# Last turns of a fused attention kernel: query product first, query norm last, hand-over and final norm rearranged

## The reference, cut to what matters

```python
# x: [32, 32, 512], ctx: [32, 257, 512]; 16 heads of 32
x = x + xattn(layernorm(x), ctx, ctx, mask)          # q/k/v/o products, softmax over 257 keys
x = x + attn(layernorm(x))                           # per sequence of 32 tokens:
#   q, k, v = split(z @ Wqkv.T + bqkv)
#   q = q / sqrt(mean(q*q) + 1e-6) * qn_w            # k likewise ("head norm")
#   out = softmax(q k^T / sqrt(32)) v ; out @ Wproj.T + bproj
z = layernorm(x)
xm = mix[0]*z_before + mix[1]*z + mix[2]*z_after     # along the sequence
h = einsum('bsd,pdm->bspm', xm, W1) + b1             # 9 experts, 128 wide
paths = einsum('bspm,pmd->bspd', h, W2) + b2
choice = argmax(tanh(xm @ Wo1 + bo1) @ Wo2 + bo2)
return x + layernorm(z + paths[choice]) * gamma + beta
```

## Time and profile before

| | us |
|---|---|
| median of 3 runs (lowest to highest) | 794.52 (793.86 to 794.61) |
| profiled execution, its own time | 793.65 |
| its span, first to last instruction | 791.7 |
| PE busy in the span | 751.6 |
| DVE, ACT, POOL busy | 390.5, 335.9, 187.7 |
| mean granted TensorE clock | 0.99 |

### The profile page before, as it was taken

One profiled execution on the slowest core, in us unless ns is written; L12 is line 12 of the kernel. 1 busy time (PEld: TensorE's weight loads), 2 busy tenths in 40 slices (PEclk: granted clock), 3 DMA queues, 4 the chain that ended last, 5 costly groups with the idle time before them and its releaser, 6 DMA issues. The chain is left out here.

```text
span 791.7 us, 20456 instructions
## 1 busy us (share of the span) xinstructions
PE 751.6 (95%) x8258; PEld 587.8 (74%) x8258; DVE 390.5 (49%) x942; ACT 335.9 (42%) x690; POOL 187.7 (24%) x245
## 2 busy tenths in 40 slices
PE   5999999999999999999999999799999989999994
PEld 4777778778877877787788777677877766677673
DVE  5544434343443344243424546756667675633546
ACT  4435444443444344444435455224554545521210
POOL 0001000010010010010100202555777770692002
PEclk9999999999999999999999999999999999999998
DMA  9211110011011101101120114120000022100011
GB/s 331 71 48 55 54 55 23 33 53 53 0 53 53 53 0 53 53 1 52 53 49 4 53 53 108 66 84 3 0 0 4 2 69 80 41 1 0 1 54 53
DMA packets 9471, 37.05 MB, mean 47 GB/s; under 512 B 2633, under 2 KB 2889, under 8 KB 6482
## 3 DMA queue, kind: packets, MB, share of 16 engines
q1 hardware_dynamic: 9426, 36.42, 13.6%
HBM read 34.32 MB, written 2.10 MB: 46 GB/s over the span
## 5 line engine op out<-in xcount | busy, mean ns | idle before, releaser
L94 PE MATMUL pj<-W_hi 128*128 128x512 f32 x512 | 209.1, 408 | 9.7 <-DVE W_lo L594 9.7
L96 PE MATMUL pj<-W_lo,W_hi 128*128 128x512 f32 x512 | 201.2, 393 | 0.0
L95 PE MATMUL pj<-W_hi,W_lo 128*128 128x512 f32 x512 | 200.4, 391 | 0.0
L94 PEld LDWEIGHTS pj<-W_hi 128*128 128x128 f32 x512 | 96.8, 189 | 40.7 <-issue 22.4
L96 PEld LDWEIGHTS pj<-W_lo,W_hi 128*128 128x128 f32 x512 | 96.7, 189 | 21.4
L95 PEld LDWEIGHTS pj<-W_hi,W_lo 128*128 128x128 f32 x512 | 97.0, 189 | 17.9
L235 POOL COPY q_b<-Q_T 128x128 f32 (+1 forms) x32 | 9.3, 291 | 415.8 <-PE tp L358 348.9
L492 ACT ACTIVATE K<-pj,bk 128x512 f32<-128x512 f32 x64 | 44.1, 690 | 136.1 <-PE pj L96 136.1
L654 DVE CUSTOM_DVE_ANT_0 m_flat<-sc,mask 128x257 f32<-128x257 f32 x64 | 25.3, 425 | 115.4 <-PE tp L358 94.1
L507 ACT ACTIVATE p_flat<-m_flat,nmax 128x257 f32<-128x257 f32 x128 | 63.8, 501 | 24.5 <-DVE nmax L654 24.5
L499 ACT ACTIVATE V<-pj 128x512 f32<-128x512 f32 x64 | 38.2, 598 | 73.7 <-PE pj L96 71.8
(11 more groups left out here) (287 smaller groups left out, 1329.3 us busy)
## 6 DMA issues: line engine op xcount, KB each, us to landing
raw<-ctx_dram SPq DMA_DIRECT2D x15, 1024.0 KB, 4.8
raw<-w_dram SPq DMA_DIRECT2D x6, 768.0 KB, 4.9
raw<-w_dram SPq DMA_DIRECT2D x4, 1024.0 KB, 4.8
x_nat<-x_dram SPq DMA_DIRECT2D x2, 1024.0 KB, 11.7
out_dram<-raw SPq DMA_DIRECT2D x8, 256.0 KB, 2.1
raw<-wk_dram SPq DMA_DIRECT2D x2, 512.0 KB, 5.4
p_flat<-ctx_dram SPq DMA_DIRECT2D x2, 512.0 KB, 6.8
m_flat<-wv_dram SPq DMA_DIRECT2D x1, 1024.0 KB, 9.9
```

Of the source, the lines that this page charges most:

```text
L94: eng.matmul(out, a_hi, b_hi, start=first, stop=False)
L95: eng.matmul(out, a_lo, b_hi, start=False, stop=False)
L96: return eng.matmul(out, a_hi, b_lo, start=False, stop=last)
```

## The change

The whole change is in the second part, from 485 us on.

1. Turns 6, 7 and NT: PE makes the query product first, then `out_proj`, then the transposes of q and k. In every turn from 2 on `z2_transposes` goes ahead of `weighted_sum`, and ACT makes `z2_hi` ahead of `o_hi`.
2. DVE: in a turn `head_norm(it-1, 0)`, the query norm, goes from behind `k_evac` to the end; the `lo` half of z2 goes ahead of `v_evac`. DVE's turns are all written out, without a loop.
3. Hand-over: `wo_proj(4)` has a PSUM bank of its own, so that neither it nor `qkv(2, 0)` waits for the bank `pw[0]` to be read; the split of the fifth weight goes earlier on ACT and on DVE (from the end of turn 1 to behind `q_evac(1)`); both head norms of tile 0 go ahead of `x1_stats(2)`.
4. Gate: `xm_hi` and `xm_lo` are made tile by tile in turns 4 to 7, `xm_lo` on DVE instead of POOL, and `g_lo` likewise on DVE.
5. Start of the experts: `spread(0)` goes ahead of the last `weighted_sum`, `out_proj(NT+2)` and both last `z3_transposes` go later, `w_split(2)`, `z3_make` and `mix_parts` take other places among the hidden rows.
6. End: the last four tiles' deviations come one by one from POOL's power; tiles 4 and 6 go through ACT (scale and shift), POOL (gamma) and an addition on POOL or DVE; tiles 5 and 7 stay on DVE. Stores follow in the order 4, 5, 7, 6.
7. Some semaphores are shared by both parts, and some are gone.

```diff
-            if isinstance(t, int) and t <= LEAD + 1:
-                return (pw[0][:, :], pw[1][:, :], pa[:, 0, :], pa[:, 1, :])[t]
+            if isinstance(t, int) and t <= LEAD + 2:
+                return (pw[0][:, :], pw[1][:, :], pa[:, 0, :], pa[:, 1, :], pa[:, 2, :])[t]
...
 # PE, body(it)
                 if has(it, -LEAD):
                     wo_proj(it + LEAD)
-                if has(it, 3):
+                    if has(it, 3):
+                        out_proj(it)
+                if not has(it, -LEAD):
+                    qkv(it, 0)
                     out_proj(it)
-                if isinstance(it, int) and it == 2:
+                    qk_transposes(it)
+                elif isinstance(it, int) and it == 2:
                     qkv(it, 0)
                     qk_transposes(it)
...
+                if not isinstance(it, int) or it >= 2:
+                    z2_transposes(it)
                 if has(it, 2):
                     weighted_sum(it)
-                if not isinstance(it, int) or it >= 2:
-                    z2_transposes(it)
...
 # PE, behind the turns
+            qkv(NT, 0)
             out_proj(NT)
             qk_transposes(NT)
-            qkv(NT, 0)
             scores(NT)
...
             hidden(1)
+            spread(0)
             weighted_sum(NT + 1)
-            spread(0)
             spread(1)
-            out_proj(NT + 2)
             hidden(2)
             spread(2)
+            out_proj(NT + 2)
+            expert(RING)
             z3_transposes(NT + 1)
-            expert(RING)
+            expert(RING + 1)
             z3_transposes(NT + 2)
...
 # ACT, body(it) and behind the turns
                 eng.activation(z2_hi[:, :, :].rearrange("p c t -> p (c t)"), pt[0][:, :], ACT.Copy).then_inc(z2hi_made, 1)
+                if has(it, 2):
+                    o2_split(it)
...
+            def xm_split_tile(u):
+                cols = slice(u * P, (u + 1) * P)
+                eng.wait_ge(mix_made, u + 2)
+                eng.activation(xm_hi[:, :, cols], O_T[:, :, cols], ACT.Copy).then_inc(xmhi, 1)
...
             choice_evac(0)
             w_split(1)
-            w_split(2)
+            spread_evac(0)
             o2_split(NT + 1)
-            z3_make(NT + 1)
-            spread_evac(0)
             hidden_split(0)
             spread_evac(1)
+            z3_make(NT + 1)
             hidden_split(1)
+            w_split(2)
+            spread_evac(2)
+            hidden_split(2)
             eng.wait_ge(proj_done, NT)
             eng.activation(b2_hi, b2, ACT.Copy).then_inc(b2_split, 1)
-            z3_make(NT + 2)
-            spread_evac(2)
-            mix_parts(NT + 1)
-            hidden_split(2)
-            w_split(3)
             spread_evac(RING)
             hidden_split(RING)
-            mix_parts(NT + 2)
-            w_split(4)
+            z3_make(NT + 2)
+            mix_parts(NT + 1)
+            w_split(3)
             spread_evac(RING + 1)
             hidden_split(RING + 1)
+            w_split(4)
+            mix_parts(NT + 2)
             w_split(5)
...
+            for t in (0, 2):
+                eng.wait_ge(shift4_made, t // 2 + 1)
+                eng.activation(y(NH + t), y(NH + t), ACT.Identity, bias=shift4[:, t:t + 1],
+                               scale=rstd4[:, t:t + 1]).then_inc(normed, 1)
...
 # DVE, the last tiles
-            y_centre(1, NH - 1)
-            y_deviations()
-            for t in (2, 3, 0, 1):
-                if t < 2:
-                    eng.wait_ge(centred, 2 * t + 2)
+            y_centre(1, 3)
+            for t in (1, 3):
+                eng.wait_ge(root_step, 2 * t + 2)
                 y_end(1, t)
+            eng.wait_ge(centred, 2)
+            eng.tensor_tensor(y(NH + 2), y(NH + 2), x_nat[:, NH + 2, :], ALU.add).then_inc(fin, 1)
```

More of the change, by code:

```diff
@@ L767, with self_attention_and_experts @@
 LEAD = 2
-def self_attention_and_experts(nc, io, out, x_nat, ident, O_T, raw, W_hi, W_lo, Wp_hi, Wp_lo, bv, bo, o_b, o_first, w_in, whi, wlo, ln3):
+def self_attention_and_experts(nc, io, out, x_nat, ident, O_T, raw, W_hi, W_lo, Wp_hi, Wp_lo, bv, bo, o_b, o_first, w_in, whi, wlo, seen, ln3):
     with ExitStack() as ctx:
@@ L962, in _ @@
                     eng.dma_start(beta, row_on_all(io["beta"])).then_inc(ln_in, 16)
-            for i, t in enumerate((0, 1, 2, 3, 6, 7, 4, 5)):
-                eng.wait_ge(fin, i + 1)
+            for t in range(NH):
+                eng.wait_ge(fin, t + 1)
+                eng.dma_start(out[t], y(t)).then_inc(stored, 16)
+            eng.wait_ge(fin0, 1)
+            eng.dma_start(out[NH], y(NH)).then_inc(stored, 16)
+            for i, t in enumerate((5, 7, 6)):
+                eng.wait_ge(fin, NH + i + 1)
                 eng.dma_start(out[t], y(t)).then_inc(stored, 16)
@@ L1084, in _, with y_root, y_scale @@
                 eng.tensor_tensor(x_nat[:, t, :], x_nat[:, t, :], beta, ALU.add).then_inc(xb_made, 1)
-            for t in range(2):
-                y_t = y(NH + t)
+            def y_root(t):
+                one = slice(t, t + 1)
                 eng.wait_ge(stats_made, NH + t + 1)
-                eng.tensor_scalar(y_t, y_t, mv4[:, t, 0:1], None, ALU.subtract).then_inc(centred, 1)
-                eng.wait_ge(centred, 2 * t + 1)
-                eng.tensor_tensor(y_t, y_t, gamma, ALU.mult).then_inc(centred, 1)
+                eng.tensor_scalar(tmp4[:, one], mv4[:, t, 1:2], LN_EPS, 1.0, ALU.add, ALU.mult).then_inc(root_step, 1)
+                eng.wait_ge(root_step, 2 * t + 1)
+                eng.tensor_tensor(rstd4[:, one], tmp4[:, one], power[:, one], ALU.pow).then_inc(root_step, 1)
+                eng.wait_ge(root_step, 2 * t + 2)
+                if t in (0, 2):
+                    eng.tensor_scalar(shift4[:, one], mv4[:, t, 0:1], rstd4[:, one], -1.0,
+                                      ALU.mult, ALU.mult).then_inc(shift4_made, 1)
+            def y_scale(t):
+                eng.wait_ge(normed, t // 2 + 1)
+                eng.tensor_tensor(y(NH + t), y(NH + t), gamma, ALU.mult).then_inc(centred, 1)
+            eng.wait_ge(fin, NH)
+            y_root(0)
+            y_scale(0)
+            y_root(1)
+            eng.wait_ge(centred, 1)
+            eng.tensor_tensor(y(NH), y(NH), x_nat[:, NH, :], ALU.add).then_inc(fin0, 1)
+            y_root(2)
+            y_root(3)
+            y_scale(2)
         @block.tensor
@@ L1116, in wo_proj @@
                     eng.wait_ge(olo_made, t - 1)
-                if has(t, LEAD + 2):
+                if has(t, LEAD + 3):
                     eng.wait_ge(qk_out, 2 * (t - LEAD - 1))
@@ L1171, in scores @@
                 need(eng, o2lo_made, u)
+                if isinstance(it, int) and it == 2:
+                    eng.wait_ge(x1_made, LEAD + 3)
                 eng.sem_inc(pe_seen, 1)
@@ L1437, in body @@
                     weight_split(2)
+                if isinstance(it, int) and it == 1:
+                    weight_split(4)
                 if has(it, 2):
@@ L1450, in body @@
                     square(it, 1)
-                if has(it, 2):
-                    o2_split(it)
-                if isinstance(it, int) and it == 1:
-                    weight_split(4)
                 eng.wait_ge(z2T_done, it + 1)
@@ L1658, in body @@
                 else:
+                    if isinstance(it, int) and it == 2:
+                        head_norm(it - 2, 0)
                     if has(it, -LEAD):
                         take_x1(it + LEAD)
+                    if isinstance(it, int) and it == 2:
+                        head_norm(it - 2, 1)
                     x1_stats(it, ch)
-                if has(it, 2):
+                if has(it, 3):
                     head_norm(it - 2, 1)
-                if has(it, 3):
                     take_x2(it)
@@ L1772, in y_end @@
                                          op0=ALU.mult, op1=ALU.add).then_inc(fin, 1)
-            steps(eng, body)
+            for it in range(NT):
+                body(it)
+                if it > NH:
+                    xm_lo_tile(it - NH - 1)
+                if it == NT - 1:
+                    eng.wait_ge(g_split, 1)
+                    eng.tensor_tensor(g_lo[:, :, :], g_raw, g_hi[:, :, :].bitcast(F32), ALU.subtract).then_inc(g_split, 1)
             ch = Chain(eng, step, count["at"])
```

115 lines of the change are left out of this document (63 added, 52 removed).

## The result

| | before | changed |
|---|---|---|
| median, us (lowest to highest) | 794.26 (793.86 to 794.61) | 798.74 (798.41 to 799.37) |
| ratio, 95% interval | | 1.0057 (1.0040 to 1.0075) |
| profiled execution, its own time; span | 793.65; 791.7 | 798.66; 797.1 |
| mean granted TensorE clock | 0.99 | 0.978 |

A forecast was written before the change was run, and what follows sets the result against it. PE, busy 751.6 of 791.7 us, bounds the span, with its idle time, lowered clock and end. Terms 2.1 + 0.4 + 1.9 - 1.1 - 2.0 + 1.0 + 3.1 = 5.4 gave 788.5 us; range 786 to 791, over all cases 783.5 to 792.5.

The forecast's parts named there:

- Clock, +3.1: PE's half-clock stretches: the one behind the spread wait goes, and one of hand-over or gate; 3.1 us gained, ends 0 and 4.6.
- Turns, +0.4: Turns 6, 7, NT: three o_lo waits go (4.3), three k_T waits come (2.9), z2's lo costs 0.5 twice; 0.4 us gained.
- Hand-over, +2.1: Turn 2: scores start at 515.9 instead of 519.6, a gain of 3.7 us, 2.1 without the clock; ends 0.5 and 3.5.
- `e_T` +1.9: PE's wait on e_T goes, as DVE makes the four tiles, one a turn; 1.9 us gained, within 1.4 to 1.9.
- gate -1.1: Before the gate PE waits 2.5 us for tile 3 of xm_lo instead of 1.4; 1.1 us lost, ends -2 and -0.6.
- Start of the experts, -2.0: Spread wait of 1.66 us goes; new waits at hidden(3), outputs(0, 0), hidden(6), spread(6) sum to 3.65; 2.0 us lost.
- End, +1.0: Last tiles' end 1.4 us shorter, less because DVE holds POOL up; 1.0 us gained, ends -0.5 and 2.
- The query's norm beside the key's power: On DVE beside POOL: the norm is not held by the power, though the skill's shared-port rule would say so.
- Rival 3: The key's power holds the query's norm like a stream; gate and turn starts lose 8.1 us, total 796; chance 0.06.
- what would show it: Signs in the trace: listed PE waits gone or new, scores at 516, a shorter end, one or two half-clock stretches, not three.

The follow-up runs named there:

- old_turns_early_b2: Changed kernel with PE's old order in turns 6, 7 and NT, and b2's lo half made ahead of take_x2 and the last tile's statistics: 786.25 us.

## Why the prediction was wrong, point by point

- **Clock, +3.1: the step that failed.** It was to give 3.1 us and took some 7.5 (an estimate: five stretches more, at the 1.5 us that the forecast reckons for one). I counted the three stretches of the earlier trace rows, asked which of them the change takes away, and never which it might bring. That each followed an idle time was read rightly; the wait that the forecast itself put before `outputs(0)` (1.5) was given no clock at all, and those at the hand-over (2) and the gate (2.5) one stretch between them. My lower end for this term was 0. `outputs(0)` alone takes 9.4 us where it took 6.3, 3.1 lost behind a wait of 1.1. The account closes with it: the five stretches and the stop of 2.8 cost 10.3; PE's other waits from 465 us on (19.3 before, 15.7 now) and the end (1.0) give back 4.6; that leaves 5.7, and the spans, 791.7 and 797.1, differ by 5.4.
- **Turns, +0.4: wrong in size by far, -6.3.** Its idle parts were right (1.42 three times gone, 0.96 three times come, `z_lo` late by 0.4 twice). The stop, 2.8, and the half clock behind it were in no case of mine. Before had one row of the kind, 0.8 in turn 3's scores, and I passed over it.
- **Hand-over, +2.1: sized within 1.5 us.** Scores come 2.2 us earlier where I had 3.7, 2.1 and 1.5 of clock: at 517.4 instead of 515.9, since the first power on the way starts at 508.5 instead of 507.6 and the second lasts 3.14. In the total the hand-over was worth 0 in the changed kernel, 0.7 and 3.6 elsewhere.
- **`e_T` +1.9 and gate -1.1: the waits right, the total short of the clock.** 0.8 forecast. By the waits it is 1.2: 2.0 and 1.3 gone, 2.1 (not 2.5) come. Measured are 2.0, and the profile has one half-clock stretch more at the old gate.
- **Start of the experts, -2.0: the mechanism right, the price wrong.** The wait before `outputs(0)` was 1.1 (1.5 forecast); those at `hidden(3)`, `hidden(6)` and `spread(6)` did not come. The wait before `gate(1)`, 1.1, I had not seen. With the clock the part cost 4.9; with b2 early it seems to gain.
- **End, +1.0: right**, 1.0 in the changed kernel and 1.1 in the pair that differs in nothing else.
- **The query's norm beside the key's power: right.** At the end of turn 6 the power runs from 602.34 to 605.24 on POOL and the norm on DVE at 603.07 takes 0.68. Rival 3 is refuted by this row; its time, 796, is nearest to the measured one for quite another reason. Where POOL streams a whole tile the norm is held: 1.66 us at 643.53, beside a POOL addition from 643.35. The Trainium skill (SBUF — State Buffer, section "SBUF: two separate sides") makes no such difference between a power and a stream; the rows do where the power comes first. Where DVE's stream came first, at 502.41, a power had to wait like anything else (2.63).

Of "what would show it", nearly all of the waits came (the one on a weight's split did not) and the number of stretches did not. With the two defects gone, old_turns_early_b2 took 786.25: the rest of the sum was not far off.

## What to carry to other kernels

A wait of 1 us in front of light work on PE (small matmuls, matmuls of 9 rows) can cost far more than itself: the one before `outputs(0)` cost 5.8 in place, since the clock fell and stayed low through all of it. Price every wait that a change adds with a half-clock stretch or more, and look for light work behind it. When a sum of terms comes out right in its waits and wrong in its time, list the stretches at half clock of both traces side by side before anything else. And undo the parts one at a time on the changed kernel: most were good, and two small edits turned a loss of 0.6% into a gain of 1.2%. When two medians differ by more than their waits do, look through the whole trace for a stretch that the edit does not touch.
